# Local attention layers: each product of weights and values issued as two halves of 32 value columns

## What is computed

```
qkv = x @ Wqkv;  q, k, v = split(qkv)           # 16 heads of 64
q, k = l2norm(q) * qs, l2norm(k) * ksc          # then rotary tables
bk2, bv2 = look(bk), look(bv)                   # each window sees itself and the one before: 64 keys
sim  = einsum('bhwie,bhwje->bhwij', bq, bk2) * 8, masked
attn = softmax(sim)
out  = einsum('bhwij,bhwje->bhwie', attn, bv2)  # the product that the change touches
return out @ Wo
```

## Time and profile before

| | |
|---|---|
| median of 3 runs | 3491.45 us (3479.96 to 3510.59) |
| the profiled execution | 3495.58 us |
| its span, first to last instruction | 3493.9 us |
| mean granted clock of PE | 0.859 |
| PE, PEld busy | 2984.6, 2097.0 us |
| DVE, ACT, POOL busy | 2049.5, 1452.7, 1470.8 us |

### The profile page before, as it was taken

One profiled execution on the slowest core, in us unless ns is written; L12 is line 12 of the kernel. 1 busy time (PEld: TensorE's weight loads), 2 busy tenths in 40 slices (PEclk: granted clock), 3 DMA queues, 4 the chain that ended last, 5 costly groups with the idle time before them and its releaser, 6 DMA issues. The chain is left out here.

```text
span 3493.9 us, 92768 instructions
## 1 busy us (share of the span) xinstructions
PE 2984.6 (85%) x38559; PEld 2097.0 (60%) x38559; DVE 2049.5 (59%) x4484; ACT 1452.7 (42%) x2511; POOL 1470.8 (42%) x1307
## 2 busy tenths in 40 slices
PE   5779999999758888888888988888888885999986
PEld 1268888889725555555555655555556563545444
DVE  5732222222138788787878787878888763534314
ACT  4622222222215555555555555555455551223333
POOL 0043333332226555655655565556555541011111
PEclk9977777777759999999999999999999996667667
DMA  0000000000021112121121112122211110000000
GB/s 27 0 6 0 0 0 0 0 0 0 15 88 46 46 39 59 47 68 42 56 65 50 55 51 67 40 59 60 55 37 48 37 48 12 1 1 1 1 1 23
DMA packets 60576, 109.23 MB, mean 31 GB/s; under 512 B 14366, under 2 KB 18734, under 8 KB 59438
## 3 DMA queue, kind: packets, MB, share of 16 engines
q1 hardware_dynamic: 59280, 102.69, 10.4%
q10 hardware_dynamic: 926, 1.27, 0.1%
HBM read 28.93 MB, written 1.05 MB: 9 GB/s over the span
## 5 line engine op out<-in xcount | busy, mean ns | idle before, releaser
L1558 POOL TENSOR_TENSOR l_rot_a<-l_rot_a,l_rot_b 128x512 f32<-128x512 f32 x384 | 484.9, 1271 | 246.7 <-DVE l_rot_b L1374 244.6
L1567 POOL TENSOR_TENSOR l_qk<-l_rot_a,l_rn 128x512 f32<-128x512 f32 x384 | 388.3, 1043 | 431.2 <-DVEq L1417 408.5
L1020 PE MATMUL l_A<-l_wts,l_H 128*128 128x512 f32 x768 | 391.4, 607 | 30.5 <-ACT l_H L1317 21.7
L1110 PE MATMUL l_T<-ident,l_qk 128*128 128x128 f32 x1536 | 229.6, 295 | 128.2 <-ACT l_qT L1274 126.3
L1243 ACT ACTIVATE l_sq<-l_A 128x512 f32<-128x512 f32 x384 | 231.1, 602 | 226.1 <-PE l_A L1020 226.0
L1368 DVE TENSOR_TENSOR l_rot_a<-l_A,l_tab 128x512 f32<-128x512 f32 x384 | 263.4, 686 | 90.3 <-ACT l_sq L1243 83.8
L1110 PEld LDWEIGHTS l_T<-ident,l_qk 128*128 128x128 f32 x1536 | 178.3, 149 | 214.0 <-issue 204.2
L1374 DVE TENSOR_TENSOR l_rot_b<-l_A,l_tab 128x512 f32<-128x512 f32 x384 | 261.0, 680 | 0.0
L1378 DVE TENSOR_REDUCE l_ss<-l_sq 128x8 f32<-128x512 f32 x384 | 259.2, 675 | 0.0
L1095 PEld LDWEIGHTS l_O<-l_pT,l_vw 64*64 64x64 f32 x9216 | 197.4, 138 | 94.3 <-ACT l_pT L1249 81.5
L1120 PEld LDWEIGHTS l_T<-l_oT,l_wts 128*128 128x128 f32 x1536 | 194.5, 198 | 54.5 <-issue 51.8
(11 more groups left out here) (345 smaller groups left out, 6160.6 us busy)
## 6 DMA issues: line engine op xcount, KB each, us to landing
l_vw<-l_vn SPq DMA_DIRECT2D x384, 128.0 KB
l_vw<-l_vn SPq DMA_DIRECT2D x360, 64.0 KB
l_wts<-in_l_wts SPq DMA_DIRECT2D x18, 650.0 KB, 5.4
l_tab<-in_l_tables SPq DMA_DIRECT2D x6, 1024.0 KB, 5.1
l_wts<-in_l_wts SPq DMA_DIRECT2D x6, 635.5 KB, 4.4
result<-x SPq DMA_DIRECT2D x4, 256.0 KB, 2.3
d_w_qkv<-in_d_w_qkv SPq DMA_DIRECT2D x1, 864.0 KB
l_scales<-in_l_scales SPq DMA_DIRECT2D x6, 128.0 KB, 5.5
```

The costliest lines, as they stand in the source:

```text
L1020: pe.matmul(A[j % 2][:], cols(m), w_of(m)[:, C_QKV + 512 * j:C_QKV + 512 * j + 512], start=True, stop=True).then_inc(pq_done, 1)
L1110: last = pe.transpose(T[c % 2][:, P * i:P * i + P], qk[:, c, P * i:P * i + P], ident[:])
L1558: pool.tensor_tensor(rot_a[m % 2][:, j, :], rot_a[m % 2][:, j, :], rot_b[:, j, :], ALU.add).then_inc(rot_rdy, 1)
L1567: pool.tensor_tensor(qk[:, j, :].rearrange("p (a d) -> p a d", d=DH), rot_a[p][:, j, :].rearrange("p (a d) -> p a d", d=DH), rn[p][:, 8 * ...
```

## The change

In `values` each call is split in two: `part` picks 32 of the 64 value columns (`VH = DH // 2`), and the result goes to 32 rows of the bank instead of 64. The loop over `part` stands outside those over bank and `e`, so that eight calls in a row go to eight different places of the array (64 rows by 32 columns each). There are 128 calls a tile instead of 64. Nothing else differs; line numbers behind the edit move by one and then by three.

```diff
+VH = DH // 2
...
                 for i in range(4):
                     for wd in range(NWIN):
-                        for bank in range(2):
-                            for e in range(2):
-                                pair, half = 4 * bank + i, e ^ bank
-                                r = slice(DH * e, DH * e + DH)
-                                if (wd, e) == (1, 0) or (wd, e) == (3, 1):
-                                    keys = vn[p][r, e, DH * pair:DH * pair + DH]
-                                else:
-                                    keys = vw[p][r, wd, DH * pair:DH * pair + DH]
-                                last = pe.matmul(O[bank][DH * half:DH * half + DH, P * i + WIN * wd:P * i + WIN * wd + WIN], keys,
+                        for part in range(2):
+                            for bank in range(2):
+                                for e in range(2):
+                                    pair, half = 4 * bank + i, e ^ bank
+                                    r = slice(DH * e, DH * e + DH)
+                                    c, row = DH * pair + VH * part, DH * half + VH * part
+                                    if (wd, e) == (1, 0) or (wd, e) == (3, 1):
+                                        keys = vn[p][r, e, c:c + VH]
+                                    else:
+                                        keys = vw[p][r, wd, c:c + VH]
+                                    last = pe.matmul(O[bank][row:row + VH, P * i + WIN * wd:P * i + WIN * wd + WIN], keys,
+                                                     pT[r, pair, WIN * wd:WIN * wd + WIN], start=True, stop=True,
+                                                     skip_group_check=True)
```

More of the change, by code:

```diff
@@ L1086, in values @@
                     for wd in range(NWIN):
-                        for bank in range(2):
-                            for e in range(2):
-                                pair, half = 4 * bank + i, e ^ bank
-                                r = slice(DH * e, DH * e + DH)
-                                if (wd, e) == (1, 0) or (wd, e) == (3, 1):
-                                    keys = vn[p][r, e, DH * pair:DH * pair + DH]
-                                else:
-                                    keys = vw[p][r, wd, DH * pair:DH * pair + DH]
-                                last = pe.matmul(O[bank][DH * half:DH * half + DH, P * i + WIN * wd:P * i + WIN * wd + WIN], keys,
-                                                 pT[r, pair, WIN * wd:WIN * wd + WIN], start=True, stop=True,
-                                                 skip_group_check=True)
+                        for part in range(2):
[11 more added lines that the diff above has]
+                                                     skip_group_check=True)
                 last.then_inc(pv_done, 1)
```

## The result

The changed kernel takes 3733.17 us (median of 4 runs, 3714.11 to 3753.28) against 3501.02 us before (4 runs, 3479.96 to 3513.64): a ratio of 1.066, 95% interval 1.0605 to 1.0715. It is slower by 232 us where 43 were forecast (78 on the path less 35 for the clock), and lies far outside the range of 3494 to 3584. The profiled execution took 3714.11 us, 218.5 more than the profiled one of before.

A forecast was written before the change was run, and what follows sets the result against it. PE and DVE handing work to each other each slot was taken to bound the kernel. From 3495.6 us, +78 for longer value products and -35 for the clock gave 3538.6, forecast as 3536 after the median adjustment; range 3494 to 3584.

The forecast's parts named there:

- What bounds the kernel: PE and DVE hand work to each other once a slot (one tile, about 19 us); PE is busy 85% of the span.
- the slack: PE's wait before the second pair of query and key transposes, 118.0 us in the stretch, could absorb longer value products.
- slot A: The tile in each group of four with the group's moments on DVE; holds about 4.1 us of PE's wait.
- The pace: Value products after the change run at the scores' pace, 2.6 us a phase instead of 1.85; bounds 1.9 and 3.7.
- Rivals 3 and 4: Respectively: half piece costs a whole one, 3556 (clock unmoved 3606), chance 0.12; 25 ns floor per record, about 3760, chance 0.01.
- The code: PE's instruction fetches stall nearly every value phase by 1.2 us, 1.1 added on average; phase 3.7 us instead of 2.1.
- The bound of 1.6: Upper bound in us on the code-fetch stall in a value phase, for a landing as late as the longest.
- The sum on the path: Slot A hides its +1.6 us; the other three slots add 3.4 us a group, over 23 groups +78 us.
- its last step: Taking off 4 us, since the median of the runs is below the profiled one: 3538.6 became 3536.
- The clock: Shorter wait in slot A avoids the fall to 1.2 GHz in four of five groups: -35 us, bounds 0 and -50.
- Rival 1: Code fetch in the value phases is hidden: +0.6 us a phase, +9 us in all, 3500 to 3505; chance 0.2.
- The signs to look for: 256 records a phase, about 10 ns pace, 1.2 us gaps, 96 more packets, slot A's wait 2 to 3 us, clock near 1.00.

The follow-up runs named there:

- the pair of placed splits: Changed kernel, split kept in one tile of four only: in slot A 3486.44 us (ratio 0.9935), in the tiles numbered 3 modulo 4 3591.05 us (ratio 1.0253).
- the block of code alone: Kernel before plus a PE-only block in front: 512 narrow calls written out, wide calls, then narrow calls in an on-chip loop; 3544.71 us in one run.
- the run with the narrow calls once: Changed kernel computing only the first half of each value product, 64 half-piece calls a tile instead of 128; 3488.82 us, ratio 0.9969 to the kernel before.

## Why the prediction was wrong, point by point

**What bounds the kernel, and the slack: right.** PE's wait ahead of the second pair of transposes was the slack of the value products, with the sizes given for slot A and the others. The changed kernel uses up all of it (118.0 to 4.2 us), and the pair of placed splits shows that it is worth what the trace says.

**The pace: right in kind, a little high.** A phase without its waits is 215.33 / 78 - 0.22 = 2.54 us of busy time, less a tail of 0.2 for each of 1.4 waits, about 2.3 us or 9 ns a record; 2.6 was forecast and 1.85 was before. Rivals 3 and 4 are out: the half piece does not cost a whole one, and 256 records at 25 ns would have been 6.4 us. The Trainium skill, TensorE: Matmul & The Clock Gate, Part 1, has such a floor between starts; for records that go to different places of the array no run here shows it, and the 9 ns speak against it.

**The code: the step that failed.** Right was that the packets are PE's code, 256 instructions each, and that the changed kernel fetches 96 more: 370 against 274, to the packet. Wrong was "the fetch of the next-but-one piece starts when one is used up", from which the stall was 2.5 - 1.3 = 1.2 us and the average 1.1. The stall that ended at 2200.78 hides nothing of the 2.3 us from fetch to resumption, and next to nothing is hidden in 61 of the 100 silences counted above; and many phases have more than one stall, 111 in 78. Measured: 2.54 us a phase, 2.4 more than before. The bound of 1.6 was wrong for the same reason. It rested on one row of q8 with its resumption, and never asked how far apart two packets can be. That answer stood in the trace of before, whose closest starts are 3.3 us apart. A phase of 512 instructions uses a packet in half the 2.6 us forecast, so no lookahead of one packet could have hidden its second. What fits three of the kernels is the distance between starts, 3.45 us, less the time that a packet's instructions take: 3.45 - 2.3 / 2 = 2.3 us for the half pieces (2.5 measured a phase), 3.45 - 4.3 / 2 = 1.3 us for the whole calls issued twice (1.5 measured a phase), and 3.45 - 1.54 = 1.9 us for the block of code alone (1.9 to 2.2). These are estimates from the rows above.

**The sum on the path.** With the measured phase: 4 x 3.0 us for the four slots, less the slack that went, 118.0 / 22 - 4.2 / 19.5 = 5.2 us, is 6.8 us for each group of four. Times 23 this is 156 us, where the prediction had 78. Slot A, which was to hide its share, is no longer free either. (The forecast itself has a slip of 1.5 us: 3538.6 less the 4 of its last step is 3534.6, not 3536. It changes nothing.)

**The clock: the sign of the term was wrong, its mechanism half right.** Behind slot A's wait the clock did come back: the value projection went from 682 to 597 ns a record, over 316 records 27 us, near the 35 forecast. But the stalls are new silences of 2 to 3 us, and the same fall now follows some of them. The windows behind the stall that ended at 2200.78, and PE's timeline there:

```profile
2201.40:2204.70 3.30, 3.30 (x52) 2.61 (x39) 0.00 (x0) 2.24 (x4) 1.76 (x1) 0.51 0.03 7
2205.00:2209.00 4.00, 4.00 (x26) 3.00 (x25) 1.88 (x3) 2.77 (x5) 1.76 (x2) 1.00 0.00 0
...
2201.75 1.97 PE L1113 MATMUL l_T<-ident,l_qk 128*128 128x128 f32 x8
...
2205.04 1.04 PE L1113 MATMUL l_T<-ident,l_qk 128*128 128x128 f32 x8
```

The first eight transposes take 1.97 us at 0.51, the second eight 1.04 at 1.00. In the phase before it a silence just as long left the clock alone:

```profile
2178.91 0.22 PE L1098 MATMUL l_O<-l_pT,l_vw 64*32 64x32 f32 x3 [2.20 <-issue]
...
2178.90:2182.00 3.10, 3.10 (x38) 2.24 (x37) 0.30 (x2) 2.68 (x6) 1.90 (x1) 1.00 0.00 0
```

Over the stretch, the groups of the kernel before and of the changed one:

```profile
L1020 PE MATMUL l_A<-l_wts,l_H 128*128 128x512 f32 x708 | 357.8, 603 | 1.2 <-issue 0.8
L1110 PE MATMUL l_T<-ident,l_qk 128*128 128x128 f32 x1408 | 210.0, 295 | 119.7 <-ACT l_qT L1274 118.0 <-issue 0.8
L1029 PE MATMUL l_O<-l_wts,l_H 128*128 128x512 f32 x356 | 196.8, 682 | 0.0
```
```profile
L1113 PE MATMUL l_T<-ident,l_qk 128*128 128x128 f32 x1264 | 227.7, 337 | 12.7 <-issue 8.2 <-ACT l_qT L1277 4.2
...
L1030 PE MATMUL l_O<-l_wts,l_H 128*128 128x512 f32 x316 | 149.9, 597 | 0.0
```

The projection lost 68 ns a record (43 us over 630), the transposes 42 (53 us over 1264), against the 27 gained: about +69 us, an upper figure since records overlap. The profiled execution is 218.5 us longer and 156 are explained by the phases, so 63 remain. The clock can fill them, and the comparison with the whole calls issued twice leaves it up to some 50. That comparison is the only run that bears on the clock's share; a part of the remainder may be something else.

**The rivals.** None described what happened. Rival 1, a hidden fetch, was the opposite of it. Rival 4's 3760 was near in time, for a reason that the run with the narrow calls once excludes. The missing case was "nothing of a fetch is hidden": 2.5 us at one boundary of each phase makes 2.6 + 2.5 = 5.1 us, the phase that was measured, and 156 us on the path, 3652 without a word on the clock. That it comes out so exactly is partly luck: the pace was 0.3 us too high, and the phases have 1.4 waits of 1.8 us and not one of 2.5.

**The signs to look for.** Seen: 256 records, a pace of about 10 ns, 96 packets, no wait left in the other slots. Seen in part: the clock behind slot A's place, where the value projection recovered. Not seen: gaps of 1.2 us, a wait of 2 to 3 us in slot A, a clock near 1.00 over the stretch.

## What to carry to other kernels

Count instructions, not only busy time, wherever a written-out stretch has many short ones: here 256 (64 calls in float32) are one packet of code that came no faster than every 3.45 us or so, and a stretch of 512 in 2.3 us waited 2.5. Before halving a piece, read the distances between code packets in the trace, and price each packet inside a burst at that distance less the time that its instructions take. Then ask where the wait will stand: the same stalls cost 2.5% ahead of one slot and nothing ahead of the slot whose slack took them.

## What the runs showed of the hardware

- Code for PE: the starts of packets were never less than 3.2 us apart, 3.45 to 3.7 in a burst of written-out calls; 2.1 to 3.1 us, in the middle 2.4, from the start of a fetch to the next instruction over the 100 silences of the changed kernel. A loop body of 256 instructions ran eight times without such a wait (10.9 ns a record). What decides when a fetch starts stays open: in the burst and behind the phase that resumed at 2200.78 it was about 1.1 us after a resumption, behind the one that resumed at 2178.91 only 3.5 us after it.
- A half piece (64 rows by 32 columns) is 1.46 us busy for 128 records where the whole piece has 2.21, with the same columns of moving data: two thirds, not half.
- The clock fell to 1.2 GHz (0.51 granted) behind a silence of 2.18 us inside the value products and stayed at 1.00 behind one of 2.20 us in the phase before. In the kernel before it fell behind one of 3.81 us and stayed behind one of 2.27 us. A silence's length alone does not tell which.
